# A four-layer mixed kernel: block rows scattered in two groups, block numbers computed first, and one group's probabilities normalised on the vector engine

## What is computed

```python
x = x + L0(x)   # paged attention: q, k, v projections, RMS norm and rotary position of q and k,
                # the new k and v written into a block cache at pos = kv_lens + t,
                # softmax over a window of 128 positions, output projection Wo
x = x + L1(x)   # einsum('bct,bcd->bdt', x, weights[conditions])
x = x + L2(x)   # the same with weights[subjects], plus a bias
x = x + L3(x)   # gated feed-forward 256 -> 1024 -> 256, silu(gate) * up, each of its three
                # linear layers with a rank-16 adapter chosen per sample
```

## Time and profile before

| what | value |
|---|---|
| median of 3 runs | 253.76 us (253.05, 253.76, 255.38) |
| the profiled execution's own time | 252.41 us |
| span from first to last instruction in it | 250.1 us |
| busy: PE / DVE / ACT / POOL | 207.7 / 143.0 / 105.2 / 70.4 us |
| DMA moved | 25.25 MB in 64124 packets |

### The profile page before, as it was taken

One profiled execution on the slowest core, in us unless ns is written; L12 is line 12 of the kernel. 1 busy time (PEld: TensorE's weight loads), 2 busy tenths in 40 slices (PEclk: granted clock), 3 DMA queues, 4 the chain that ended last, 5 costly groups with the idle time before them and its releaser, 6 DMA issues.

```text
span 250.1 us, 5105 instructions
## 1 busy us (share of the span) xinstructions
PE 207.7 (83%) x1995; PEld 187.9 (75%) x1995; DVE 143.0 (57%) x494; ACT 105.2 (42%) x291; POOL 70.4 (28%) x82
## 2 busy tenths in 40 slices
PE   2699978475865769959899799999979999899995
PEld 1577867364655658949789789888978988799994
DVE  5749878557656747285636644743664454326522
ACT  2163337656740573158323634632363463213310
POOL 3420047330038750176270443227040022000000
PEclk9999999859779999979999999999999999999999
DMA  6787899927983378899794012002200000010001
GB/s 167 219 173 110 187 190 239 320 73 160 136 222 93 105 182 120 195 202 190 130 156 111 3 42 66 0 3 73 76 1 3 0 3 0 3 42 3 0 3 42
DMA packets 64124, 25.25 MB, mean 101 GB/s; under 512 B 55780, under 2 KB 60836, under 8 KB 63524
## 3 DMA queue, kind: packets, MB, share of 16 engines
q1 hardware_dynamic: 60432, 14.07, 28.4%
q0 software_dynamic: 2944, 10.23, 16.1%
q10 hardware_dynamic: 724, 0.62, 0.8%
HBM read 17.83 MB, written 7.08 MB: 100 GB/s over the span
## 4 chain that ended last, share of the span: by engine, by line
PE 31%; issue 15%; DVE 13%; POOL 10%; DMA 5%; ACT 5%; SPq 4%; POOLq 1%
PE bank L1451 26%; POOL far L662 5%; SPq L542 4%; DMA early<-in_kb,blk_i 4%; POOL prob L676 3%; DVE prob L1084 3%; ACT prob L793 3%; DMA d_raw<-in_Wd 2%; DVE mask L1063 1%; PE bank L1437 1%; POOL near L665 1%; PE bank L1417 1%; POOL prob_near L677 1%; PE bank L1398 1%; DVE gs L1133 1%
## 5 line engine op out<-in xcount | busy, mean ns | idle before, releaser
L662 POOL DMA_INDIRECT far<-table_rows,place_i x32 | 31.5, 983 | 70.8 <-issue 37.2
L793 ACT ACTIVATE prob<-prob,ntop,qscale 128x160 f32<-128x160 f32 x64 | 32.4, 508 | 17.1 <-DVE ntop L1090 17.1
L1451 PE MATMUL bank<-xf_high,gu_high 128*128 128x256 f32 x128 | 39.1, 305 | 0.0
L1451 PE MATMUL bank<-xf_high,gu_low 128*128 128x256 f32 x128 | 36.3, 284 | 0.0
L1451 PE MATMUL bank<-xf_low,gu_high 128*128 128x256 f32 x128 | 36.3, 283 | 0.0
L1133 DVE SCALAR_TENSOR_TENSOR gs<-th,bank 128x256 f32<-128x256 f32 x32 | 13.4, 419 | 27.3 <-ACT th L828 27.0
L676 POOL TENSOR_TENSOR prob<-prob,rden 128x512 f32<-128x512 f32 x12 | 12.7, 1055 | 48.6 <-DVE rden L1109 48.6
L1451 PEld LDWEIGHTS bank<-xf_high,gu_high 128*128 128x128 f32 x128 | 24.6, 192 | 1.4 <-issue 1.0
L1451 PEld LDWEIGHTS bank<-xf_low,gu_high 128*128 128x128 f32 x128 | 24.5, 191 | 0.2
L1451 PEld LDWEIGHTS bank<-xf_high,gu_low 128*128 128x128 f32 x128 | 24.4, 191 | 0.0
L828 ACT ACTIVATE th<-bank 128x256 f32<-128x256 f32 x32 | 12.0, 380 | 24.3 <-PE bank L1451 24.3
(11 more groups left out here) (224 smaller groups left out, 523.2 us busy)
## 6 DMA issues: line engine op xcount, KB each, us to landing
table_rows<-early SPq DMA_DIRECT2D x32, 144.0 KB
table_rows<-far_probs SPq DMA_DIRECT2D x2, 512.0 KB, 3.6
gu_raw<-in_Wg SPq DMA_DIRECT2D x2, 512.0 KB, 5.2
gu_raw<-in_Wu SPq DMA_DIRECT2D x2, 512.0 KB, 5.7
d_raw<-in_Wd SPq DMA_DIRECT2D x2, 512.0 KB, 4.7
out<-xs SPq DMA_DIRECT2D x8, 128.0 KB, 1.9
xs<-in_x ACTq DMA_DIRECT2D x1, 512.0 KB, 5.0
xs<-in_x SPq DMA_DIRECT2D x1, 512.0 KB, 5.7
```

The source lines that it names most:

```text
L662: pool.indirect_dma_start(far[r][:, s, :], None, seen, bass.IndirectOffsetOnAxis(ap=far_i[:, GB * n + s:GB * n + s + 1], axis=0)).then_inc ...
L793: last = act.activation(v, v, ACT.Exp, bias=ntop[r][:, j:j + 1], scale=qscale[:, n, j:j + 1], accum_out=den[r][:, j:j + 1])
L1451: last = pe.matmul(dst, w[a], x[b], start=start and n == 0, stop=stop and n == 2)
```

## The change

It has five parts.

1. `scatter_rows` goes by groups: the 72 rows of a tile are laid out as 2 x 36 (group, block, sample), and each scatter is 16 DMAs of 36 partitions x 16 pieces, first k and v of the first group, then k and v of the second, each half with a semaphore of its own. The table shrinks to one place per group, used again by every tile, with the new rows between them. So a scatter of tile `t` first waits until all gathers of tile `t - 1` have landed (`next_rows`).
2. `prepare` of an even group waits for the first half alone; of an odd group for both.
3. SP's order: the scatter of tile 2 moves behind the down weights `d0`, `d1` and so behind the wait for `mixer_psum` 2.
4. The start: DVE takes only 8 of 12 bits first, shifts the table, makes `own_blk` and lets PE turn it alone; `blk_i` follows. The positions and the other small products come after `blk_i`.
5. In FIRST_ORDER, ("den", 0) goes, and ("norm0", 0) stands before `up1`, ("norm1", 0) behind it: group 2's probabilities are normalised by DVE in two halves. Groups 3 to 7 stay with POOL.

The diff, cut (constants of the layout and the renamed DRAM offsets left out):

```diff
-     ("scores", 0), ("mask", 1), "gate1", ("first", 1), "up1", ("den", 0), ("prod", 1), "gate2", "up2",
+     ("scores", 0), ("mask", 1), "gate1", ("first", 1), ("norm0", 0), "up1", ("norm1", 0), ("prod", 1), "gate2", "up2",
...
             def scatter_rows(t):
+                for half in range(2):
+                    lo = int(HALF_AT[half])
+                    own = slice(half * HB, (half + 1) * HB)
+                    for raw, come, at in ((k_raw, k_in, 0), (v_raw, v_in, KH)):
+                        sp.wait_ge(come, 16 * (t + 1))
+                        for g in range(G):
+                            sp.dma_start(table_rows[lo:lo + HALF_ROWS, at + g * HD:at + (g + 1) * HD].rearrange(
+                                "(p o) d -> p o d", o=BLOCK),
+                                raw[own, g * BLOCK * HD:(g + 1) * BLOCK * HD].rearrange("p (o d) -> p o d", d=HD)
+                            ).then_inc(rows_out[t][half], 16)
+
+            def next_rows(t):
+                for r in R:
+                    sp.wait_ge(kv_in[r], 16 * (GB + 1) * t)
+                scatter_rows(t)
...
-            scatter_rows(1)
+            next_rows(1)
             gate_up("g1", Wg, 0, upper)
             gate_up("u1", Wu, 1, upper)
-            next_rows(2)
             sp.wait_ge(mixer_psum, 2)
             for half in range(2):
                 sp.dma_start(d_raw[...
+            next_rows(2)
             sp.wait_ge(ssum_ready, SUMS)
...
             def load_blocks(t):
+                if t:
+                    for half in range(2):
+                        pool.wait_ge(rows_out[t - 1][half], 16 * 2 * G)
...
             def prepare(n, r):
-                pool.wait_ge(k_out[t], 16 * G)
-                pool.wait_ge(v_out[t], 16 * G)
+                for half in range(r + 1):
+                    pool.wait_ge(rows_out[t][half], 16 * 2 * G)
                 pool.wait_ge(new_out, 32)
...
         @block.vector
-            for k in range(12):
+            for k in range(11, 3, -1):
                 dve.tensor_scalar(bits[:, k:k + 1], len_i[:, 0:1], k, 1, ALU.logical_shift_right, ALU.bitwise_and)
-            then(dve.tensor_scalar(len_i[:, 1:2], len_i[:, 0:1], BLOCK - 1, None, ALU.bitwise_and))
-            then(dve.tensor_copy(len_f[:, 0:2], len_i[:, 0:2]))
-            dve.wait_ge(k32_in, 16)
-            dve.tensor_scalar(four_len[:, :], c3("four"), len_f[:, 0:1], None, ALU.mult)
-            dve.tensor_scalar(diag_len[:, :], c3("eye32"), len_f[:, 0:1], None, ALU.mult).then_inc(pos_ready, 1)
             dve.wait_ge(tab_in, 16)
...
             then(dve.tensor_copy(blk[:, :], tab_f[:, 0:SLOTS]))
-            dve.tensor_tensor(own_blk[:, :, :], over(blk[:, :], 2, BT), over(c3("eighth"), 1, SLOTS), ALU.mult)
-            dve.tensor_tensor(wblk[:, :, :], over(blk[:, BACK:SLOTS], 1, B), over(c3("eye32"), 2, WS), ALU.mult
+            dve.wait_ge(k32_in, 16)
+            dve.tensor_tensor(own_blk[:, :, :, :], over(over(blk[:, 0:OLD], 1, 2), 3, GB),
+                              over(c3("eighth").rearrange("s (h b) -> s h b", h=2), 2, OLD), ALU.mult
                               ).then_inc(slot_ready, 1)
+            dve.tensor_tensor(wblk[:, :, :], over(blk[:, BACK:SLOTS], 1, B), over(c3("eye32"), 2, WS), ALU.mult)
+            dve.tensor_scalar(len_i[:, 1:2], len_i[:, 0:1], BLOCK - 1, None, ALU.bitwise_and)
+            for k in range(3):
+                dve.tensor_scalar(bits[:, k:k + 1], ...
+            then(dve.tensor_scalar(bits[:, 3:4], ...
             dve.wait_ge(slot_psum, 1)
             dve.tensor_copy(blk_i[:, :], small("slots", BP)).then_inc(blk_ready, 1)
+            then(dve.tensor_copy(len_f[:, 0:2], len_i[:, 0:2]))
+            dve.tensor_scalar(four_len[:, :], c3("four"), len_f[:, 0:1], None, ALU.mult)
+            dve.tensor_scalar(diag_len[:, :], c3("eye32"), len_f[:, 0:1], None, ALU.mult).then_inc(pos_ready, 1)
+            dve.wait_ge(slot_psum, 2)
...
         @block.tensor
+            pe.wait_ge(slot_ready, 1)
+            pe.matmul(small("slots", BP), own_blk[...], c3("tile"), start=True, stop=True).then_inc(slot_psum, 1)
             pe.wait_ge(pos_ready, 1)
+            pe.matmul(small("writer", NW)[:, 0:2], wblk[...], ones[0:B, 0:2], start=True, stop=True)
             pe.matmul(small("writer", NW)[:, 2:4], c3("spread_writer"), len_f[:, 0:2], start=True, stop=True)
             pe.matmul(small("pos"), c3("spread_four"), four_len[:, :], start=True, stop=True)
             pe.matmul(small("lens"), ones[0:B, :], diag_len[:, :], start=True, stop=True)
-            pe.wait_ge(slot_ready, 1)
-            pe.matmul(small("slots", BP), ...
-            pe.matmul(small("writer", NW)[:, 0:2], ...
             pe.matmul(wblk_rows, ...).then_inc(slot_psum, 1)
```

More of the change, by code:

```diff
@@ L34 @@
 BK = BT * OLD
-BP = BT * SLOTS
+HB = GB * OLD
+BP = 2 * HB
 BACK = WINDOW // BLOCK
@@ L42 @@
 NEW_ROWS = B * T
-TILE_ROWS = BK * BLOCK
-TILE_AT = np.array([0, TILE_ROWS + B * T])
+HALF_ROWS = HB * BLOCK
+HALF_AT = np.array([0, HALF_ROWS + NEW_ROWS])
 FF = 1024
@@ L113, in tables @@
     j, o = np.arange(WIDTH)[None, :] // BLOCK, np.arange(WIDTH)[None, :] % BLOCK
-    put(c, C32, "own", (np.minimum(j, OLD - 1) * BT + s % BT) * BLOCK + o + TILE_AT[s // BT % 2])
+    put(c, C32, "own", (np.minimum(j, OLD - 1) * GB + s % GB) * BLOCK + o + HALF_AT[s // GB % 2])
     return a, b, c
@@ L165 @@
 MIX_BANKS = ((1, 1), (0, 2))
-SMALL = {"slots": (0, 0, NT), "writer": (0, 4, 8), "later": (0, 8, 24), "pos": (7, 0, NG), "lens": (7, 32, 64), "subj": (6, 64, 96),
+SMALL = {"slots": (0, 0, NT), "writer": (6, 4, 8), "later": (0, 8, 24), "pos": (7, 0, NG), "lens": (7, 32, 64), "subj": (6, 64, 96),
          "scale": (6, 96, 224), "rows": (0, 224, 224 + WIDTH), "place": (0, 400, 400 + B + NG), "bias": (0, 440, 448),
@@ L267, in build @@
         blk = sb("blk", [B, SLOTS])
-        own_blk = sb("own_blk", [B, SLOTS, BT])
+        own_blk = sb("own_blk", [B, 2, OLD, GB])
         wblk = sb("wblk", [B, B, WS])
@@ L395, in build @@
         v_in = sem("v_in")
-        k_out = [sem(f"k_out{t}") for t in range(NT)]
-        v_out = [sem(f"v_out{t}") for t in range(NT)]
+        rows_out = [[sem(f"rows_out{t}_{half}") for half in range(2)] for t in range(NT)]
         new_out = sem("new_out")
@@ L550, in new_rows @@
                 sp.wait_ge(k_ready, half + 1)
-                lo = TILE_ROWS + half * NEW_ROWS // 2
+                lo = HALF_ROWS + half * NEW_ROWS // 2
                 sp.dma_start(table_rows[lo:lo + NEW_ROWS // 2, :].rearrange("(g p) c -> p g c", p=P),
@@ L634, in load_blocks @@
             def load_blocks(t):
-                for dst, src, seen, done in ((k_raw, kb, k_out, k_in), (v_raw, vb, v_out, v_in)):
-                    if t:
-                        pool.wait_ge(seen[t - 1], 16 * G)
+                if t:
+                    for half in range(2):
+                        pool.wait_ge(rows_out[t - 1][half], 16 * 2 * G)
+                for dst, src, done in ((k_raw, kb, k_in), (v_raw, vb, v_in)):
                     pool.indirect_dma_start(dst, None, src.rearrange("n g o d -> n (g o d)"),
-                                            bass.IndirectOffsetOnAxis(ap=blk_i[0:BK, t:t + 1], axis=0)).then_inc(done, 16)
+                                            bass.IndirectOffsetOnAxis(ap=blk_i[:, t:t + 1], axis=0)).then_inc(done, 16)
             pool.wait_ge(blk_ready, 1)
@@ L997, in _ @@
             won, own = small("rows", B), c3("own")
-            then(dve.scalar_tensor_tensor(moved_by[:, :], won, float(TILE_ROWS - 1), own, ALU.add, ALU.subtract))
+            then(dve.scalar_tensor_tensor(moved_by[:, :], won, float(HALF_ROWS - 1), own, ALU.add, ALU.subtract))
             then(dve.scalar_tensor_tensor(moved_by[:, :], won, 0.0, moved_by[:, :], ALU.is_gt, ALU.mult))
@@ L1210, in _ @@
             pe.wait_ge(ones_set, 1)
+            pe.wait_ge(slot_ready, 1)
+            pe.matmul(small("slots", BP), own_blk[:, :, :, :].rearrange("s h j b -> s (h j b)"), c3("tile"), start=True,
+                      stop=True).then_inc(slot_psum, 1)
             pe.wait_ge(pos_ready, 1)
+            pe.matmul(small("writer", NW)[:, 0:2], wblk[:, :, :].rearrange("s w n -> s (w n)"), ones[0:B, 0:2],
+                      start=True, stop=True)
             pe.matmul(small("writer", NW)[:, 2:4], c3("spread_writer"), len_f[:, 0:2], start=True, stop=True)
@@ L1214, in _ @@
             pe.matmul(small("lens"), ones[0:B, :], diag_len[:, :], start=True, stop=True)
-            pe.wait_ge(slot_ready, 1)
-            pe.matmul(small("slots", BP), own_blk[:, :, :].rearrange("s j b -> s (j b)"), c3("tile"), start=True, stop=True)
-            pe.matmul(small("writer", NW)[:, 0:2], wblk[:, :, :].rearrange("s w n -> s (w n)"), ones[0:B, 0:2],
-                      start=True, stop=True)
             pe.matmul(wblk_rows, ones[0:B, 0:NW], wblk[:, :, :].rearrange("s w n -> s (w n)"), start=True, stop=True
```

14 lines of the change are left out of this document (6 added, 8 removed).

## The result

The changed kernel takes 260.08 us (median of 4 runs, 259.83 to 260.15), the kernel before 254.57 us beside it (4 runs). The ratio is 1.0235, with a 95% interval of 1.0175 to 1.0295: slower by 2.4%, where 248.7 us were forecast. The profiled execution has a span of 258.3 us against 250.1. The medians lie 5.5 us apart and the two profiled spans 8.2, because the kernel before was profiled in a short execution (252.41 us); so some 2 us of the 8.2 are not the change's.

A forecast was written before the change was run, and what follows sets the result against it. First pass bound not by PE but by full DMA engines and waits, around group 3 by DVE and ACT; second pass by PE. +0.75 - 1.45 - 1.9 - 3.0 + 0.5 = -5.1 us from 253.76 gives 248.7 us, range 247 to 250.5.

The forecast's parts named there:

- 1: SP's scatter in halves: an issue of 36 partitions costs 0.54 us, 16 issues 8.6 us as before; bounds 0.41 and 1.07.
- 2: Start on DVE and PE: `blk_i` 2.0 us earlier but the k chain later; +0.75 us, within 0 and +1.2.
- 3: Gathers of group 2: the 2.59 us stall before `kt` goes, but late `b1` leaves only 1.45 us gained.
- 4: Group 2 normalised by DVE in halves: `pv` finishes earlier, gain 1.8 to 1.9 us, between 0 and 2.9.
- 5: Down weights before tile 2's scatter on SP: the 2.87 us stall before group 3's scores goes; 3.0 us gained.
- 6: Adapter `ad` behind the scatter in SP's queue: there at 111.8 us, barely late, +0.5 us, between 0 and 3.5.
- 7: Waits added before the scatters of tiles 1, 2 and 3: cost 0, tile 3's with 4 us to spare.
- Rival A: SP's queue: each half-size transfer costs what a whole one did, 1.07 us x 16; slower, 257.7 us; chance 0.06.

The follow-up runs named there:

- mended version: Changed kernel with the adapter DMAs issued ahead of tile 2's scatter and group 3 also normalised by DVE in halves: 248.0 us, ratio 0.9713.

## Why the prediction was wrong

Step by step, as it numbered them:

1. **The price of a halved issue is the step that failed.** I took 0.54 us for 36 partitions, because whole issues of 1152 and 1024 pieces cost the same per piece. It is 0.76 us at the least, 0.82 and 0.92 on average over tiles 1 and 2. I read 1.07 us per whole transfer as a price per piece; under it lies a floor per issue. The run with halved scatters alone, and those with 24 and 32 partitions, show it. The adapter's row was no such price either: with the down weights first, the same eight issues have a median of 0.62 us, against 0.84 in the trace before. That a full queue made them 1.06 us on average is argued. The trace before had the hint: the same group of issues has a minimum of 783 ns where adapter issues with nearly as many pieces have 508. I had the bounds of 0.41 and 1.07 right, and chose by the wrong row.
2. The start was right: forecast +0.75, measured +0.6 at `kt` of group 0, `blk_i` 2.0 us earlier, `later_same` 0.8 us later; alone it costs 0.85 us, just clear of noise.
3. The gathers of group 2 started at 70.43 us (forecast 69.8), and `b1` was late behind them as foreseen. But the 8.0 us from first gather to landed rows were wrong: in the mended version they are 11.2 (70.73 to 81.94), and PE waits 2.95 us there; with the adapter first they are 11.7, and PE waits 3.35 us. With whole scatters they are 7.7 to 9.3 us in six profiles, and 8.5 with halved scatters alone, where the gathers wait for all sixteen. So the halves start the gathers some 2 us earlier, and the rows land no earlier: at 81.9 and 82.0 us, against 79.9 to 82.2. The second half of the scatter is issued while the first half's rows are gathered. Only where the two overlap is the time above 9.3 us; that they hold each other up is argued from that, and no run was made for it. In the changed kernel itself PE came late enough not to wait.
4. The normalising gained 1.8 us in its own stretch where it was alone, and 1.8 in the mended kernel (83.7 to 94.8), but 1.1 in the changed kernel (84.7 to 96.5), where the granted clock of that stretch was 0.86; the step was right. It is worth nothing while the down weights come late.
5. The down weights first: right for the stall (gone in every version that has it).
6. **The adapter is where the error of step 1 was paid.** The sum said landed at 111.8; it was 123.5. Down weights were issued 4.0 us late (92.47, after a first pass that began late). Tile 2's scatter took 14.8 us; I gave 8.6 to 9.4 and put 8.6 into the sum. The adapter's last issue began 6.7 us after its first where I counted 8.45, and it landed after 8.0 us, not 4.6: +4.0 + 6.2 - 1.9 + 3.4 = 11.7, with 0.2 us for the down weights and rounding in the -1.9. Even whole scatters take 11.9 and 11.7 us behind the down weights, so 8.6 was too low for the new order at any price of the halves. The long landing falls together with POOL's loads of tile 3, issued at 112.25 and 113.51, in a stretch with a DMA share of 1.10; where the adapter went first, the median landing was 2.7 us, against 5.5 here. I had bounded the issue at 0.75 us and the lateness at 3.5; my own upper bound of 1.07 in step 1 would have given 8.5.
7. The added waits cost PE nothing in any version. But tile 3's scatter came at 141.0 us, not at 120: `pv` of group 3 was late, at 130.6, and the gathers of group 5, for which I took no time, fill the 10 us between. In the mended kernel the same gap runs from 119.7 to 131.6 us.

A term was missing altogether: with the down weights ahead, POOL's product of group 3 stands behind gathers that wait for the scatter. In the run with the down weights first alone it takes back all of step 5. In the changed kernel it costs 0.66 us: its gathers begin at 104.89 us, behind the first half of the scatter, against 108.58 in that run, behind a whole one. That is the one place where the halves pay.

Rival A had the mechanism and the place, and got 0.06. The price was 0.76 to 0.92 us and not 1.07, and its deciding point, "about 1.0 us per issue", was wrong: at 0.92 the kernel was already 5.5 us slower, because I let everything else in that sum, the start of the down weights and the landing, keep its best value. (A's sum also has a slip: 118.5 + 3.6 is 122.1, not 121.3.)

## What to carry to other kernels

A row that gives 1.07 us for a large transfer is no price per piece: look at the minimum and the median of the issues, and cut a transfer only when half its price is still above the smallest issue of that form. Before a step is moved in an in-order queue, list everything behind its last landing on every engine: here the adapter on SP and a product on POOL, where moving the adapter alone moved the wait to the product, and undoing both was worth 12 us. And try an outer size that divides by 16: 80 rows with 11% more data had the cheaper median issue, and three of four scatters were shorter than with 72.

## What was not expected of the hardware

- A scatter issue on SP that goes over 12 DMA engines has a floor of 762 ns, the same for 36 partitions with 576 pieces and for 24 with 384 (783 for 72 with 1152). Over 16 engines the smallest issues take 626 and 562 ns with 32 partitions, and 558 with 80.
- One profile to the next, the first feed-forward pass began up to 5 us apart with the same code ahead of it (73.0 and 78.0 us).
